# Turning normed feature maps to pixel rows on 64x64 TensorE tiles, the norm's factor applied after the turn

## What is computed

```python
x = x + _L0_conv_ref(_gn(x), ...)   # shifted-window attention, then a feed-forward part
x = x + _L1_conv_ref(_gn(x), ...)   # the second norm, and the second layer:
...
xb = x.reshape(n, c, LRF, LH, LRF, LW).transpose(2, 4, 0, 1, 3, 5)
xb = xb.reshape(NB, n, c, L)                      # 16 blocks of 64 pixels
scores = jnp.einsum('gbcl,gc->gbl', xb, conv_w)
e = jnp.exp(scores)
p = e / jnp.sum(e, axis=-1, keepdims=True)
_, idx = jax.lax.top_k(p, K)                      # K = 6
mask = jnp.sum(jax.nn.one_hot(idx, L, dtype=p.dtype), axis=2)
st = jax.lax.stop_gradient(mask - p) + p
out = st[:, :, None, :] * xb
gath = jnp.take_along_axis(out, jnp.sort(idx, axis=-1)[:, :, None, :], axis=-1)
feat = jnp.concatenate([gath.transpose(0, 1, 3, 2).reshape(NB, n, K * c), st], axis=-1)
h = jax.nn.relu(feat @ W1 + b1)
rec = h @ W2 + b2
...
```

## Time and profile before

| what | value |
|---|---|
| median of 3 runs | 780.2 us (779.53 to 784.32) |
| span of the profiled execution | 778.6 us, 21192 instructions |
| mean granted TensorE clock, of full speed | 0.923 |
| PE busy, DVE busy, ACT busy | 86%, 66%, 62% of the span |
| drain and the block's end | about 622 to 677.8 us |

### The profile page before, as it was taken

How to read it: one execution, slowest core, us unless ns; L and a number is a source line. 1 busy time by engine, 2 the same in 40 slices (tenths; PEclk the granted TensorE clock), 3 DMA queues, 4 the chain that set the end, 5 groups by cost and what they waited for, 6 DMA issues and landing times. The chain is left out here.

```text
span 778.6 us, 21192 instructions
## 1 busy us (share of the span) xinstructions
PE 665.7 (86%) x8584; PEld 371.4 (48%) x8584; DVE 516.4 (66%) x997; ACT 480.4 (62%) x963; POOL 355.1 (46%) x441
## 2 busy tenths in 40 slices
PE   4785789999999999999998579999999988749880
PEld 2562455565565555655555232233333367735350
DVE  4796487877777787877778322577777786372181
ACT  3565266777777777777775548877777656624000
POOL 4696446778777777788776520022221123100000
PEclk9787599999999999999999959999999999969955
DMA  9550000000000000000000020122112220120278
GB/s 216 137 128 11 1 3 2 3 2 3 2 3 3 3 3 3 3 2 3 3 2 3 2 56 1 28 55 56 33 50 55 55 55 2 31 72 2 63 194 269
DMA packets 15719, 31.44 MB, mean 40 GB/s; under 512 B 7488, under 2 KB 9284, under 8 KB 15620
## 3 DMA queue, kind: packets, MB, share of 16 engines
q1 hardware_dynamic: 12592, 29.16, 14.1%
q10 hardware_dynamic: 2760, 0.66, 0.5%
q0 software_dynamic: 272, 0.27, 0.2%
HBM read 20.71 MB, written 9.37 MB: 39 GB/s over the span
## 5 line engine op out<-in xcount | busy, mean ns | idle before, releaser
L794 POOL TENSOR_TENSOR sc<-sc,mx 128x512 f32<-128x512 f32 x128 | 133.7, 1044 | 102.4 <-DVE mx L725 102.4
L722 DVE TENSOR_TENSOR sc<-s_ps,bias_tab 128x512 f32<-128x512 f32 x128 | 87.7, 685 | 52.6 <-PE s_ps L528 52.6
L1424 POOL TENSOR_TENSOR square<-xs 128x1024 f32<-128x1024 f32 x16 | 34.1, 2133 | 165.5 <-DVE xs L1166 165.5
L539 PE MATMUL t_ps<-consts,sc 128*128 128x128 f32 x512 | 84.4, 288 | 16.2 <-ACT pt L656 12.5
L656 ACT ACTIVATE pt<-t_ps 128x512 f32<-128x512 f32 x128 | 75.7, 592 | 31.2 <-PE t_ps L539 30.1
L539 PEld LDWEIGHTS t_ps<-consts,sc 128*128 128x128 f32 x512 | 54.3, 142 | 84.8 <-issue 48.1
L725 DVE TENSOR_REDUCE mx<-sc 128x8 f32<-128x512 f32 x128 | 87.8, 686 | 4.4
L1081 ACT ACTIVATE hs<-h_ps,fb1s 128x512 f32<-128x512 f32 x128 | 78.2, 689 | 19.1 <-PE h_ps L990 19.0
L528 PE MATMUL s_ps<-kx,qu 32*64 32x128 f32 x2048 | 72.3, 278 | 3.5 <-DVE kx L749 2.9
L990 PE MATMUL h_ps<-xs,fw 64*128 64x512 f32 x256 | 68.7, 650 | 1.0 <-ACT hs L1081 1.0
L528 PEld LDWEIGHTS s_ps<-kx,qu 32*64 32x64 f32 x2048 | 56.7, 134 | 15.2 <-issue 13.4
(11 more groups left out here) (207 smaller groups left out, 1295.2 us busy)
## 6 DMA issues: line engine op xcount, KB each, us to landing
raw<-in_x_dram SPq DMA_DIRECT2D x32, 256.0 KB, 5.1
xr<-in_x_dram SPq DMA_DIRECT2D x32, 256.0 KB, 3.9
out_dram<-x SPq DMA_DIRECT2D x32, 256.0 KB, 3.9
rec_scratch<-r SPq DMA_DIRECT2D x4, 224.0 KB, 2.5
w<-in_L_conv_W_dram SPq DMA_DIRECT2D x1, 784.0 KB
w<-in_L_conv_W_dram SPq DMA_DIRECT2D x1, 672.0 KB
xs<-rec_scratch SPq DMA_DIRECT2D x16, 28.0 KB
xs<-rec_scratch ACTq DMA_DIRECT2D x16, 28.0 KB
```

The costliest lines, as they stand in the source:

```text
L539: last = pe.transpose(t_ps[:, m], sc[n % KEPT][:, m].rearrange("c h k -> c (h k)"), ident)
L722: dve.tensor_tensor(sc[n % KEPT][:, :, :, :], s_ps[j][:, :, :, :], bias_tab[:, j, hp], ALU.add)\
L794: pool.tensor_tensor(v, v, mx[n % KEPT][:, :].unsqueeze(2).broadcast_to([128, 8, TOK]), ALU.subtract)\
```

## The change

A job's matmuls go to 64x64 tiles: for each group of 128 pixels, each of the two 64-pixel blocks and each of the two images has a matmul of its own, with 64 rows, 64 stationary columns and 66 moving columns (16 matmuls a job, 32 PE instructions, where there were 8). `turn` shrinks to [128 x 66] and needs no zeros. The result is copied to yt unscaled, by ScalarE alone, in one ACTIVATE a job of 2 x 264 columns; VectorE copies no job. The factors of all pairs are computed in one batch, late: `turn_var` after 29 jobs, `spread_pixels` after 31. VectorE copies them to a tile `factors` and multiplies the scores by them (`own_scores`), at the end of the block instead of the copies at the tail's start. TensorE also transposes the factors in the tail, and one more VectorE instruction multiplies the selection weights by them (cr). The table preload at L1660 goes. The order of `tensor_drain` is written anew: 21 jobs stand before the last pair's mean, where 14 stood, and 11 behind it, where 18 stood; the third place is used from job 16 on.

```diff
-            EARLY = 10
-            BATCHES = ((0, EARLY), (EARLY, PAIRS))
             JOBS = 2 * PAIRS
+            LATE = 16
...
-                return j % 2 if j < 2 * EARLY else j % 3
+                return j % 2 if j < LATE else j % 3
...
+            def turn_var(pe):
+
+                pe.wait_ge(s["sqsum"], PAIRS)
+                pe.wait_ge(s["out"], UNITS)
+                pe.wait_ge(s["csq"], UNITS)
+                for p in range(PAIRS):
                     last = pe.matmul(c_ps[0:W, 2 * p:2 * p + 2], sqsums[:, p], spread_image[:, 0:128:C], start=True, stop=True)
...
+            def spread_pixels(pe):
+
+                pe.wait_ge(s["turn_rstd"], 2)
                 for e in range(2):
+                    last = pe.matmul(pixel_factors(e), to_pixels[:, e], turn_rstd[:, :], start=True, stop=True)
...
                 for n in range(4):
                     gp = 4 * half + n
-                    last = pe.matmul(TURN_BANKS[turn_place(j)][:, n // 2, TURN * (n % 2):TURN * (n % 2 + 1)],
-                                     xs[:, p, 128 * gp:128 * (gp + 1)], turn[:, gp], start=True, stop=True)
+                    for b, (to_lo, to_hi) in enumerate(HALVES):
+                        px = slice(128 * gp + TOK * b, 128 * gp + TOK * (b + 1))
+                        for a, (lo, hi) in enumerate(HALVES):
+                            last = pe.matmul(TURN_BANKS[turn_place(j)][to_lo:to_hi, a, SIDE * n:SIDE * (n + 1)],
+                                             xs[lo:hi, p, px], turn[lo:hi, gp], start=True, stop=True)
...
             def take_turned(act, j):
-                act.wait_ge(s["pixel_rstd"], 1 if j < 2 * EARLY else 2)
                 act.wait_ge(s["turned"], j + 1)
+                to = yt[:, j // 2, 4 * (j % 2):4 * (j % 2 + 1)].rearrange("c g a n -> c a g n")
+                act.activation(to, TURN_BANKS[turn_place(j)][:, :, 0:4 * SIDE].rearrange("c a (g n) -> c a g n", g=4),
+                               ACT.Copy).then_inc(s["taken"], 1)
+
+            def own_scores(dve):
+
+                dve.wait_ge(s["pixel_ps"], 1)
                 for e in range(2):
-                    for a in range(2):
-                        last = act.activation(turn_blocks(j, e)[:, :, a], turn_fill(j)[:, :, e, a], ACT.Copy,
-                                              scale=pixel_rstd[:, e, j // 2, a:a + 1])
-                last.then_inc(s["turn_a"], 1)
...
+                    dve.tensor_copy(factors[:, :, :, e], pixel_factors(e).rearrange("c (p a) -> c p a", a=2)
+                                    .unsqueeze(2).broadcast_to([128, PAIRS, 4, 2]))
+                dve.wait_ge(s["taken"], JOBS)
+                blocks = yt.rearrange("c p (y e) a n -> c p y e a n", e=2)
+                for b, (lo, hi) in enumerate(HALVES):
+                    for e in range(2):
+                        factor = pixel_factors(e)[lo:hi].rearrange("c (p a) -> c p a", a=2)
+                        dve.tensor_tensor(scores[lo:hi, :, :, e], blocks[lo:hi, :, :, e, :, C + b],
+                                                 factor.unsqueeze(2).broadcast_to([C, PAIRS, 4, 2]), ALU.mult)
...
-                    for j in range(2 * EARLY, JOBS, 2):
-                        multiply_turned(dve, j)
+                    own_scores(dve)
...
-                    turn_rstds(act, 0)
-                    for j in range(2 * EARLY):
+                    for j in range(JOBS - 3):
                         take_turned(act, j)
-                    turn_rstds(act, 1)
-                    for j in range(2 * EARLY + 1, JOBS, 2):
+                    turn_rstds(act)
+                    for j in range(JOBS - 3, JOBS):
                         take_turned(act, j)
...
-                    for b, (lo, hi) in enumerate(HALVES):
-                        last = dve.tensor_copy(scores[lo:hi], yt[lo:hi, :, :, :, C + b])
-                    last.then_inc(s["own"], 1)
...
+                    dve.wait_ge(s["factor_rows"], 1)
+                    link(dve.tensor_tensor(cr[:, :, :], st[:, :, :], psb[3][:, 0:256].rearrange("c (t l) -> c t l", t=4),
+                                           ALU.mult))
...
-                    act.preload_act_table_set(EXP_LN)
...
+                    for t in range(2):
+                        last = pe.transpose(psb[3][:, 128 * t:128 * (t + 1)],
+                                            factors[:, 8 * t:8 * t + 8].rearrange("c p y e a -> c (p y e a)"), ident)
+                    last.then_inc(s["factor_rows"], 1)
```

More of the change, by code:

```diff
@@ L944, in build @@
         iota_in = sem(whole, "iota_in")
+        scores = sb(whole, "scores_sb", [128, PAIRS, 4, 2, 2])
+        factors = sb(whole, "factors", [128, PAIRS, 4, 2, 2])
         yt = flat[:, 0:PAIRS * 8 * TURN].rearrange("c (p g a n) -> c p g a n", p=PAIRS, g=8, a=2)
@@ L949, in build @@
                 "rstd_ps", "scaled", "update", "placed", "sum_ps", "sums", "mean", "centred", "square", "sq_ps", "sqsum",
-                "turn_var", "turn_rstd", "pixel_ps", "pixel_rstd", "turned", "turn_a", "turn_b")}
+                "turn_var", "turn_rstd", "pixel_ps", "pixel_rstd", "turned", "taken")}
             FORWARD_LINKS = 6
             SETS = UNITS // 4
-            turn = sb(stage, "turn", [128, 8, TURN])
+            turn = sb(stage, "turn", [128, 8, SIDE])
             cw_in = sb(stage, "cw_in", [128, BLOCKS])
@@ L1218, in turn_var, with pixel_factors @@
+            def turn_var(pe):
[3 more added lines that the diff above has]
+                for p in range(PAIRS):
                     last = pe.matmul(c_ps[0:W, 2 * p:2 * p + 2], sqsums[:, p], spread_image[:, 0:128:C], start=True, stop=True)
                 last.then_inc(s["turn_var"], 1)
-            def spread_pixels(pe, b):
-                first, last_pair = BATCHES[b]
-                pe.wait_ge(s["turn_rstd"], 2 * b + 2)
+            def pixel_factors(e):
+                return c_ps[:, 64 * (e + 1):64 * (e + 1) + 2 * PAIRS]
@@ L1234, in turn_job @@
                 if j == 0:
-                    pe.wait_ge(s["zero"], 5)
+                    pe.wait_ge(s["zero"], 4)
                 if j < 2:
                     pe.wait_ge(s["gelu"], 4 * UNITS)
-                elif turn_place(j) == 2 and j < 2 * EARLY + 3:
-                    pe.wait_ge(s["scaled"], UNITS)
-                else:
-                    taken(pe, max(i for i in range(j) if turn_place(i) == turn_place(j)))
+                else:
+                    earlier = [i for i in range(j) if turn_place(i) == turn_place(j)]
+                    if earlier:
+                        pe.wait_ge(s["taken"], earlier[-1] + 1)
+                    else:
+                        pe.wait_ge(s["scaled"], UNITS)
@@ L1261, in take_turned, with turn_rstds @@
+                last.then_inc(s["turned"], 1)
+            def turn_rstds(act):
+                act.wait_ge(s["turn_var"], 1)
+                act.activation(turn_rstd[:, :], c_ps[0:W, 0:2 * PAIRS], ACT.Ln, bias=eps[0:W, 0:1])\
+                   .then_inc(s["turn_rstd"], 1)
+                act.wait_ge(s["turn_rstd"], 1)
+                act.activation(turn_rstd[:, :], turn_rstd[:, :], ACT.Exp, scale=-0.5).then_inc(s["turn_rstd"], 1)
             def take_turned(act, j):
-                act.wait_ge(s["pixel_rstd"], 1 if j < 2 * EARLY else 2)
@@ L1297, in tensor_drain @@
                 spread_rstd(pe, 7, 0)
-                spread_pixels(pe, 0)
+                turn_jobs(1)
                 pair_mean(pe, 6, 0)
-                turn_jobs(1)
+                turn_jobs(2)
                 pair_square_sum(pe, 5, 1)
@@ L1318, in tensor_drain @@
                 pair_mean(pe, 7, 1)
+                turn_jobs(2)
+                pair_square_sum(pe, 7, 0)
+                turn_jobs(5)
+                pair_square_sum(pe, 7, 1)
                 turn_jobs(1)
-                pair_square_sum(pe, 7, 0)
+                turn_var(pe)
+                turn_jobs(2)
+                spread_pixels(pe)
                 turn_jobs(1)
[L1322 to L1327, removed]
+                assert next(job, None) is None
             def tensor_step(pe, n):
@@ L1400, in _ @@
                 def _(pool):
-                    pool.memset(turn[:, :, :], 0.0).then_inc(s["zero"], 1)
-                    pool.wait_ge(s["zero"], 1)
                     pool.wait_ge(s["w_in"], 32)
[L1404 to L1407, removed]
-                    last.then_inc(s["zero"], 1)
[L1409 to L1414, removed]
+                    for lo, hi in HALVES:
+                        pool.tensor_copy(turn[lo:hi, :, 0:C], ident[lo:hi, lo:hi].unsqueeze(1).broadcast_to([C, 8, C]))\
+                            .then_inc(s["zero"], 1)
+                    pool.wait_ge(s["zero"], 2)
+                    last = pool.tensor_copy(turn[:, :, C:SIDE], cw_in[:, :].rearrange("c (g b) -> c g b", b=2))
+                    last.then_inc(s["zero"], 1)
+                    pool.wait_ge(s["zero"], 3)
                     for e in range(2):
@@ L1500, in build @@
```

(4 more changed lines are left out.)

48 lines of the change are left out of this document (9 added, 39 removed).

## The result

The changed kernel takes 775.09 us (median of 5 runs, 773.67 to 777.36) where the kernel before takes 781.79 in the runs of the same comparison. The ratio is 0.9917 with a 95% interval of 0.9896 to 0.9937: faster by 0.8%, some 6.5 us, about half of the 13.6 us forecast. The interval does not reach 1, but the gain is under the one per cent that the prediction had set as the bound of "same". The two profiled spans, 778.6 and 771.9 us, differ by 6.7.

The account below looks back on a forecast made before the run. Bound: the drain, by VectorE's list, then ScalarE and finally TensorE. Drain 14.5 + tail 0.6 - clock 1.5 = 13.6 us off 778.6 gives 765.0; plus 1.6 for earlier runs' median, 766.6 us; range 763 to 775.

Parts of the forecast that it names:

- same: Outcome class for the whole kernel: within one per cent, 7.8 us (772.4 to 788.0), of the span; chance 0.18.
- What bounds the kernel: Feed-forward drain, two stretches: VectorE's list nearly closed in the first; ScalarE before 665, then TensorE in the second.
- The job's price on TensorE: Drain's jobs: 32 instructions at 14 ns make 0.45 us, taken as 0.47, against 0.90 today.
- rival A: Drain's jobs: loads set the pace, 27 ns an instruction, 0.86 us a job; time 772.6 us; chance 0.18.
- rival B: Drain's jobs: tiles don't run beside each other, 56 ns an instruction, 1.79 us a job; time 797.7 us; chance 0.05.
- First stretch: Drain up to the last pair's centring: 2.5 us of VectorE's waits gone, ending at 653.9 against 656.44.
- the last centring where it was: Sign of a wrong prediction, in the drain: the last centring stays in place instead of ending near 654.
- Second stretch: Last centring to drain's end: TensorE's list of 7.29 us, then copy and products; end 663.1 against 677.57, 14.5 us.
- ScalarE: Drain's copies: one Copy of 528 columns a job, 0.61 us for 1.16; binds nowhere unless a copy costs over 0.95.
- Tail: After the drain: start 1.05 us shorter, cr costs 0.45, net 0.6 us gained; everything behind shifts as it is.
- Clock: In the drain: today's lower level costs some 1.7 us and stays; 1.5 us (0 to 4) added for a further dip.
- Rival C: Drain: short bursts keep the granted clock at 1.2 GHz throughout, only the tail's 0.6 us gained; 779.6 us; chance 0.10.

Follow-up runs that it names:

- after_again: The changed kernel again, unchanged, run on the same chip as two follow-up kernels: 774.32 us, ratio 0.9891 to the kernel before.
- e3_mix: Against the changed kernel, every other job (the odd ones) is a wide job on the whole array, the rest on 64x64 tiles: 773.40 us, ratio 0.9897.
- The two mixes: Changed kernel with some jobs on the whole array: e3_mix, and one with jobs 0, 1, 11 to 13, 23, 24, 28 wide, in runs (771.89 us).
- e2_split: Against the changed kernel, each 64x64 matmul is cut into two of 33 columns, twice the instructions for the same columns: 802.31 us (one run).
- e4_rows: Against the changed kernel, only rows are split: 64 rows, 128 stationary and 66 moving columns, 8 matmuls a job: 808.16 us, ratio 1.0352 to the kernel before.

## Why the prediction was wrong, step by step

**What bounds the kernel.** Right: the drain's two stretches, with TensorE's list at the end of both, and nothing outside of them changed by more than half a microsecond.

**The job's price on TensorE.** The array's price was right, 0.47 us in a row, and with it the choice of the L557 row over L528; the mechanisms of rivals A and B are out. The step that failed is taking that price as the job's price in TensorE's list, "nine jobs at 0.47 = 4.23" and "7 x 0.47": from above only the load was considered, and I never asked whether instructions come that fast. A job in a row costs 1.0 us, since it needs 64 of the 256 instructions of a block, at 3.7 to 4.0 us a block. The rows were there to warn: with 32 matmuls and 32 loads a job the changed drain has some 2,500 PE instructions in 45 us, and from 636.00 to 656.60 they run at 62 a us. In the kernel before, 20 us of attention (200 to 220) hold 364 matmuls and 367 loads, 37 a us; the streams of the earlier trace rows are bursts of 8 to 64 matmuls. With 1.0 in place of 0.86, the sum of rival A has the products' end at 656.4 + 13.9 = 670.3; measured 670.03. (A small slip in rival B: the 48 us of today are 677.57 - 630.4 = 47.2. Nothing hangs on it.)

**First stretch.** Forecast 29.4 us, measured 31.9 against 32.0 before: the whole 2.5 us are missing, and the prediction's own sign of being wrong, "the last centring where it was", came true. The forecast had left today's dip of the clock in, and it was the same: 0.83 over 10 us before is 3.4 us at the lower level, 0.97 over 10 and 0.65 over 4 after are 0.6 + 2.8. What ate the gain is the supply. From 636.00 to 656.60 the row of windows has 642 matmuls and 634 loads, 5.0 blocks; at 4.0 us a block that is 19.9 of the 20.6 us. The stops of 0.50 and 0.59 us are where it shows, in front of a fold of squares (1.50) and of the last mean (1.57). After_again, with no dip, took 30.2; the forecast's own 1.7 for the dip taken off, its sum would be 27.7, so 2.5 are missing there too.

**Second stretch.** Forecast 9.2 us from centring to the end of the products, measured 670.03 - 656.60 = 13.4. Stops of 0.22, 1.95 and 0.47 make 2.6 of the difference; the products took 1.33 for 1.05. The rest, 1.3, was not taken apart; changes of shape at 0.17, which the sum had only as an overlap, and PE's wait for the centring are in it. The supply alone gives nearly the whole stretch: 356 + 356 instructions are 2.8 blocks, 11.1 us of the 11.4 to the end of PE's last job (667.29 + 0.70). The gain was 7.7 us, not 12.

**ScalarE.** Right: 0.61 a job, idle ahead of most copies.

**Tail.** The start is 1.5 us to the sum where 2.1 stood, with no table load, 0.6 shorter and not 1.05: VectorE stood 0.40 before the sum ("issue"), for a reason that no view shows. Cr costs its 0.43. The whole came out 0.4 longer, not 0.6 shorter; the first stream of gathering took 2.49 us in this profile for 2.02 before. The eight profiles with the new tail lie between 84.2 us (e3_mix) and 85.5 (after_again), around the single 84.6 of the kernel before: the gain of 0.6 is not shown, and none of them reached 84.0.

**Clock.** The allowance of 1.5 us for a further dip was not needed in the changed kernel's profile: the first stretch had as much of the lower level as before, and behind the centring, at 0.95, the jobs keep their 0.70 us to the last. In after_again, with 0.78 from 656 to 671, the second stretch took 14.6 us for 13.7. Rival C is out as it was written, for the clock did not stay low.

**The numbers.** The time, 775.09, lies 0.09 above a range that ended at 775.0; the range counted a slower job but took each term's cause from the array. Of the 8.5 us between 766.6 and 775.09, 1.6 are not the change's: the kernel before has its median at 781.79 in five runs and had it at 780.2 in three. The other 6.9 are the gain of 6.7 in place of 13.6. With 1.0 us a job the sum of rival A gives a gain of 6.4, near the measured one, but in part by luck: its 1.5 for the clock was not needed, and its 0.6 gained in the tail came out as 0.8 lost, with the end.

## What to carry to other kernels

Small tiles multiply instructions: count them, loads too, and hold them against the rate at which the engine gets them, here 256 in about 4 us, before the array's rate is believed. Stops inside a group of equal instructions, with "issue" as their releaser and the same count between them, are the mark. Where both forms of a step exist, mix them in runs rather than one by one: the wide ones give the supply time, and each change of shape costs. The two mixes here differ also in how many jobs are wide (16 and 8), so what the runs alone are worth is not shown.

## What the runs showed of the hardware that was not expected

- Instructions of PE came at one block of 256 per 3.7 us (e2_split) to 4.0 us (changed kernel); single stops lasted from 0.2 to 1.95 us in the changed kernel, up to 2.1 in e2_split.
- Matmuls of 66 columns on 64x64 tiles follow each other at 15 ns with a load each; on the four column tiles of L557, with 64 columns, it is 14.
- A change of the tile's shape between jobs cost some 0.17 us (e3_mix).
- A stream of 64-row, 128-column tiles with 66 moving columns left the granted clock at 0.50 for over 60 us, with PE busy 63.1 of 65 us from 640 to 705 (e4_rows). Why it didn't rise there, and does with the other two forms, was not tried.
